# The last slot of x loaded as one transfer of 96 partitions and four of eight, in a two-stage conditioned residual kernel

## What is computed

```python
def cond(x, index, weights):
    w = weights[index]                       # (128, 64, 64)
    return jnp.einsum('bct,bcd->bdt', x, w)

x = x + cond(x, itok_B_0_7, L0_cond_weights)
x = x + cond(x, itok_B_1_198, L1_cond_weights)
return x
```

## Time and profile before

| | us |
|---|---|
| time, median of 3 runs (lowest, highest) | 92.53 (92.41, 93.13) |
| time of the profiled execution | 92.66 |
| its span, first to last instruction | 90.8 |
| outside the span (92.66 less 90.8) | 1.9 |
| PE busy, share of the span | 77.9, 86% |
| DVE busy | 60.3, 66% |
| ACT busy | 57.0, 63% |
| POOL busy | 23.3, 26% |
| bytes moved by DMA | 35.93 MB, mean 396 GB/s |
| queue q1 (x), share of 16 DMA engines | 46.5% |
| queue q10 (stores, w0_rows), share of 16 DMA engines | 45.9% |

### The profile page before, as it was taken

How to read it: one execution, slowest core, us unless ns; L and a number is a source line. 1 busy time by engine, 2 the same in 40 slices (tenths; PEclk the granted TensorE clock), 3 DMA queues, 4 the chain that set the end, 5 groups by cost and what they waited for, 6 DMA issues and landing times.

```text
span 90.8 us, 2462 instructions
## 1 busy us (share of the span) xinstructions
PE 77.9 (86%) x907; PEld 44.2 (49%) x907; DVE 60.3 (66%) x126; ACT 57.0 (63%) x114; POOL 23.3 (26%) x119
## 2 busy tenths in 40 slices
PE   0799949995999999999999999999999999995000
PEld 0688939994454544544544364454436444440000
DVE  2295007995288788887888887788879688788100
ACT  2999705886267677765767685676758577577000
POOL 3400019989999889100000000000000000000000
PEclk9999999999999999999999999999999999999965
DMA  2999999999999999999999999999999999999992
GB/s 51 303 419 440 440 365 411 417 408 408 406 419 402 406 410 406 413 426 415 422 413 417 420 408 430 411 424 419 411 422 413 426 417 422 411 419 422 419 406 112
DMA packets 9311, 35.93 MB, mean 396 GB/s; under 512 B 594, under 2 KB 724, under 8 KB 9172
## 3 DMA queue, kind: packets, MB, share of 16 engines
q1 hardware_dynamic: 4370, 16.78, 46.5%
q10 hardware_dynamic: 4786, 16.91, 45.9%
q0 software_dynamic: 144, 2.10, 5.4%
HBM read 19.01 MB, written 16.78 MB: 394 GB/s over the span
## 4 chain that ended last, share of the span: by engine, by line
PE 68%; DMA 11%; DVE 9%; issue 3%; DVEq 1%; POOL 1%; POOLq 0%
PE psum L235 58%; DMA w_rows<-in_L_cond_weights_dram,cond 11%; DVE w L279 7%; PE psum L216 7%; PE psum L257 2%; DVEq L75 1%; DVE xy L313 1%; PE psum L196 1%; DVE m_diag L286 0%; POOL ident L150 0%; POOLq L161 0%; DVE w_rows L380 0%; POOL ident L148 0%; POOLq L150 0%; DVEq L285 0%
## 5 line engine op out<-in xcount | busy, mean ns | idle before, releaser
L235 PE MATMUL psum<-xy,m_diag 64*128 64x512 f32 x240 | 53.4, 595 | 0.0
L313 DVE COPY xy<-psum 64x512 f32<-64x512 f32 x60 | 41.0, 683 | 11.1 <-PE psum L235 10.2
L313 ACT COPY xy<-psum 64x512 f32<-64x512 f32 x60 | 34.9, 581 | 17.6 <-PE psum L235 16.9
L235 PEld LDWEIGHTS psum<-xy,m_diag 64*128 64x128 f32 x240 | 22.8, 187 | 25.5 <-issue 24.8
L169 POOL COPY w0b<-w0t 64x64 f32 x112 | 21.5, 235 | 10.9 <-DMA w_rows<-in_L_cond_weights_dram,cond 9.0
L279 ACT COPY w<-psum 64x256 f32<-64x256 f32 x16 | 5.8, 364 | 4.7 <-PE psum L196 3.6
L216 PEld LDWEIGHTS psum<-w,w0b 64*32 64x32 f32 x512 | 5.6, 105 | 6.4 <-issue 3.0
L186 PE MATMUL psum<-ident,w_rows 128*64 128x128 f32 x54 | 8.3, 331 | 0.0
L196 PE MATMUL psum<-ident,w_rows 128*64 128x128 f32 x64 | 7.2, 274 | 1.2 <-DVE w_rows L380 1.2
L186 PEld LDWEIGHTS psum<-ident,w_rows 128*64 128x64 f32 x54 | 7.4, 139 | 0.8
L196 PEld LDWEIGHTS psum<-ident,w_rows 128*64 128x64 f32 x64 | 7.0, 151 | 1.5 <-DVE w_rows L380 1.5
(11 more groups left out here) (18 smaller groups left out, 8.8 us busy)
## 6 DMA issues: line engine op xcount, KB each, us to landing
xy<-in_x_dram SPq DMA_DIRECT2D x15, 1024.0 KB, 20.5
out_dram<-xy ACTq DMA_DIRECT2D x14, 1024.0 KB, 14.1
out_dram<-xy ACTq DMA_DIRECT2D x4, 512.0 KB, 7.8
xy<-in_x_dram SPq DMA_DIRECT2D x2, 512.0 KB, 6.2
w_rows<-in_L_cond_weights_dram ACTq DMA_DIRECT2D x1, 128.0 KB, 2.2
cond_row<-in_itok_B_dram SPq DMA_DIRECT2D x1, 0.5 KB
subjects<-in_itok_B_dram ACTq DMA_DIRECT2D x1, 0.5 KB
w_rows<-in_L_cond_weights_dram,cond POOLq DMA_INDIRECT x1, 10.0
```

The lines of the kernel that those rows point to most:

```text
L235: last = nc.tensor.matmul(psum[:, 2 * (s % Y_RING) + h, :], m_diag[rows, odd, v % M_RING, j, :], xy[rows, s, j * T:(j + 1) * T], start=j = ...
L313: copy(xy[rows, s, i * T:(i + 1) * T], psum[HALVES[i], 2 * (s % Y_RING) + h, :]).then_inc(done, 1)
```

## The change

SP's last transfer, unit 15 as 1 MB, is replaced by six: slot 30 as 512 KB with all 128 partitions, the first 96 partitions of slot 31 (384 KB), and the last 32 partitions of slot 31 in four transfers of 8 partitions (32 KB each). PE's wait for unit 15 asks for all six (96 instead of 16). Nothing else differs.

```diff
+    APART = P // 4
+    FEW = 8
...
+        loaded = [16] * UNITS
+        loaded[1] = 32
+        loaded[UNITS - 1] = 32 + 16 * (APART // FEW)
...
-            for v in range(2, UNITS):
+            for v in range(2, UNITS - 1):
                 load(2 * v, 2)
+            load(SLOTS - 2, 1)
+            sp.dma_start(xy[:P - APART, SLOTS - 1, :], x_view[:P - APART, SLOTS - 1, :]).then_inc(s_x[UNITS - 1], 16)
+            for q in range(P - APART, P, FEW):
+                sp.dma_start(xy[q:q + FEW, SLOTS - 1, :], x_view[q:q + FEW, SLOTS - 1, :]
+                             ).then_inc(s_x[UNITS - 1], 16)
...
-                    pe.wait_ge(s_x[v], 32 if v == 1 else 16)
+                    pe.wait_ge(s_x[v], loaded[v])
```

## The result

| | before | after |
|---|---|---|
| median of 22 runs each, us | 92.56 | 92.87 |
| lowest, highest | 92.33, 93.13 | 92.67, 93.98 |
| ratio, 95% interval | | 1.0034 (1.0018 to 1.0050) |
| profiled execution, its span | 92.66, 90.8 | 92.77, 91.0 |

The change makes the kernel slower by 0.34%, 0.31 us, with an interval of 0.17 to 0.46 us. That is inside the 1% that I had called "within", and clear of zero. The two profiled executions lie only 0.11 us apart, so a single pair of profiles could not have shown it; the medians do.

What follows compares the result with a forecast made beforehand. The prediction took the backlogged DMA engines, not PE, to bound the kernel; the packet shift's expected +0.2 us, with tiny packets, SP's issues and stores at 0, moved the median from 92.53 to 92.7 us, range 92.1 to 93.1.

Steps and rivals of the forecast that it cites:

- within: Whole kernel's time: a move of less than 1% (0.93 us) either way, given a chance of 0.90.
- What bounds the kernel: End of the kernel: DMA engines always have a backlog, so the last engine to finish sets the end, not PE.
- Step (1): Slot 31's loads: eight engines get 10 packets, the rest 6, against 8 each; 0.31 us more or less work.
- The sum: End of the kernel: chances of where late engines stand give 0.16 + 0.04 + 0.01 = +0.2 us; bounds +0.05 and +0.36.
- Step (2): Ends of the new loads: five more tiny packets on each of the eight engines; taken as 0, at most 0.05 us.
- Step (3): SP's queue after 33.4 us: five more issues take 2 to 19 us, hidden by 13 us of slack, costed at 0.
- The group rival: End of the stores: all late engines are among those with fewer packets; -0.31 us, to 92.2; chance 0.25.
- Nothing moves: End of the kernel: small transfers take different engines, or late engines change from run to run; 92.5 us; chance 0.19.
- The crowding rival: Small loads into SBUF: eight neighbouring partitions share a way in, up to 1.9 us more; 93.0 to 94.7; chance 0.08.
- Engines 7 and 15: End of the stores: these engines are usually slower and 7 is among the eight, so the full +0.31 us, to 92.8.

Runs made afterwards that it cites:

- probe_low: Kernel before plus tiny loads of 1 to 6 rows behind the last store; PE's clock fell early, last store issued at 87.1 us, engines ended within 0.2 us.
- Double: Kernel before with slot 31 as 64 rows plus eight transfers of 8 rows, twice the change's shift; 93.41 against 92.55 us, ratio 1.0092.
- relief4: Kernel before with slot 31 as 112 rows plus four transfers of 4 rows; 92.53 against 92.56 us, ratio 0.9994.
- probe_low2: Kernel before plus tiny loads of 1 to 6 rows behind the last store, clock whole; last store issued at 84.2 us, engine 4 ended last at 90.67 us.
- probe_before: Kernel before plus tiny loads of 6, 7, 8, 14, 15 and 16 rows behind the last store; engine 14 ended last at 90.375 us.
- few4: Kernel before with slot 31 as 96 rows plus eight transfers of 4 rows; 93.02 against 92.62 us, ratio 1.0040.
- many16: Kernel before with slot 31 as eight transfers of 16 rows and slot 30 by itself, no shift; 92.70 against 92.64 us, ratio 1.0011.
- all16: Kernel before with slot 31 as 64 rows plus four transfers of 16 rows, no shift; 92.76 against 92.55 us, ratio 1.0017.
- early: Kernel before with the change's split applied to unit 5 (slots 10 and 11) in place of unit 15; 95.09 against 92.64 us, ratio 1.0245.

## Why the prediction was right, and where not

*What bounds the kernel.* Right. The last store was issued half a microsecond earlier and landed 0.2 us later; probe_low shows the opposite case.

*Step (1), two packets more on eight engines.* Right in count (642 and 4418 as forecast). Double, with twice the shift, cost +0.85 us, and relief4, with as many transfers but the packets laid on other engines, cost nothing; so the cost goes with which engines get the packets.

*The sum.* I forecast +0.2 us as a mean over where the late engines stand, within +0.05 to +0.36; measured are +0.31 us, 0.17 to 0.46, which holds both my mean and the full +0.31 of two packets. The probes don't decide between them: the last engine of the kernel before was among the eight in one of two undisturbed executions, as the 0.50 had it, and the end would have moved by 0.31 us there and by 0.17 in the other. The step that I read wrongly is the spacing of the late engines. I took their ends from the packets, the second 0.15 us ahead of the last. By the semaphore raises, which are what the program waits for, the two were 0.03 us apart in that execution, so either of them among the eight gives nearly the full rise (0.31 or 0.29 us). With the same chances, 0.50 for the last and 0.27 for the second alone, and 0.20 for only the third or fourth (+0.08 us), that makes about +0.25 us instead of +0.2. A clear rise had three chances in four by these raises; how near the median came to the full 0.31 us may be partly luck.

*Step (2), tiny packets.* 0.006 us each, 0.03 us for five; within the bound of 0.05.

*Step (3), SP.* Right that it is hidden: the last of the six transfers landed at 66.6 us, some 12 us before PE first needs slot 30. The 2 to 19 us forecast for five more issues were 8.9 us.

*The group rival* (the rest late, -0.31 us). Refuted as a group by the sign of the change and by probe_low2, where the two last raises were 0.34 us apart and the last was number 4's. A single engine of the rest, number 14, was last in probe_before. *Nothing moves*: refuted by the interval.

*The crowding rival.* Absent in the change, so its 0.08 did no harm, but my evidence against it was of the wrong kind. I argued from stores of 64 rows, which read SBUF, and from engines being out of step. Splitting a slot in a stretch of loads alone costs 2 us, by whatever mechanism. Had the change stood at slot 11, I would have been wrong by 2.2 us.

*Engines 7 and 15.* By the Trainium skill's row ("DMA: Bandwidth & Descriptors", "Latency and other measured facts") I had given the full +0.31 through engine 7, and left out that the row calls the lateness specific to software-made descriptors. Engine 7 was not late in any trace that numbers it. Where the last engine could be numbered it was 4, 14, and one of the first six. few4 and relief4 agree that it isn't one of the first four. Why an engine is late, and whether some are late more often than others, stays open.

## What to carry to other kernels

When the DMA share is over 1.0 up to the last microseconds, as it was here, the end belongs to the DMA engine that finishes last, and a change is to be counted in packets per engine: two packets of 4 KB more on half of the engines were 0.31 us here, and PE finishing earlier was worth nothing. Before splitting a transfer to balance engines, find out which engine is late, and in more than one execution: here it was a different one in two of them. Tiny transfers of 1, 2, 3 ... rows behind the last store number the engines, if the raises of the last store are read beside them. And try a split at its own place: the same rows taken out of a 128-row load in a stretch of loads alone cost 2 us, beside stores, and without a shift, the loss was too small to tell from nothing.

## What the runs showed that I had not expected

- Splitting one slot into transfers of 96 + 32 rows in a stretch of loads alone raised the time of a 4 KB packet from 0.16 to about 0.3 us for some 5 us, with the DMA share near 1.0 throughout, for 1.8 us in all; beside stores splits without a shift cost 0.06 and 0.2 us (many16 and all16), not told from nothing.
- A DMA share of 1.0 doesn't mean full rate: in early it stayed at 0.92 to 1.15 while the rate fell to 172 GB/s.
- Which DMA engine ends last changes between executions: number 4 by 0.34 us in probe_low2, number 14 by 0.14 us in probe_before. In the profiled execution of all16, which shifts nothing, one engine ended 0.82 us behind the next (91.117 against 90.295 us), and that execution took 93.37 us, 0.6 above its median.
- A tiny load of 32 bytes per row behind a store costs an engine 0.15 to 0.20 us, while a tiny packet that ends a transfer costs 0.006 us.
- PE's granted clock fell to about half early in two of the profiled executions (slices seven and eight, or eight alone); the last store then went out 2 to 3 us late, and that of double took only 0.1 us more than its median all the same. That the backlog took up the rest is my reading; the late clock and the longer wait before it were not told apart.
